# Attention and quantised feed-forward on one core: row maxima first in SyncE's list, stores and stack loads behind them and earlier, first stack in two halves, bulk loads issued by ScalarE

## The reference, cut to what matters

```python
# x, ctx: (16, 64, 256) f32; 8 heads of 8 channels; softmax over the 256 positions
def xattn(q, k, v, gamma):
    qh, kh, vh = (a.reshape(16, 8, 8, 256) for a in (q, k, v))
    qk = einsum('bhdq,bhdl->bhql', qh, kh) / sqrt(8)
    return gamma * einsum('bhql,bhdl->bhdq', softmax(qk), vh).reshape(16, 64, 256)

x = x + xattn(layernorm(x), ctx, ctx, gamma)          # k and v are both ctx
a = layernorm(x)                                      # (1024 rows, 256)
h = silu(bit_linear(a, w_gate)) * bit_linear(a, w_up) # (1024 rows, 1024)
h = rms_norm(h, ln_weight)
x = x + bit_linear(h, w_down)                         # (1024 rows, 256)
# bit_linear: activations rounded to 8 bits by their row's maximum,
# weights rounded to -1, 0, 1 by the mean of their absolute values
```

## Time and profile before

| what | value |
|---|---|
| median of 3 runs | 244.86 us (244.29 to 246.13) |
| span of the profiled execution | 248.6 us |
| busy PE, DVE, ACT, POOL | 178.4, 151.6, 140.9, 107.3 us |
| mean granted TensorE clock | 0.890 |
| DMA moved | 19.95 MB, mean 80 GB/s |

### The profile page before, as it was taken

The page is one execution under the profiler, slowest core; times in us unless marked ns, Lnnn a source line. Parts: engine busy times, 40 slices in busy tenths (PEclk is TensorE's granted clock), DMA queues, the critical chain, the costliest instruction groups (busy, mean ns, idle before and its releaser), DMA issues.

```text
span 248.6 us, 4308 instructions
## 1 busy us (share of the span) xinstructions
PE 178.4 (72%) x1370; PEld 103.8 (42%) x1378; DVE 151.6 (61%) x282; ACT 140.9 (57%) x286; POOL 107.3 (43%) x282
## 2 busy tenths in 40 slices
...
PEclk9999999996599997997569999965995699999689
...
GB/s 100 139 142 261 126 177 313 115 121 154 63 1 37 118 107 0 56 149 77 1 67 141 75 26 116 135 9 34 142 105 0 5 3 22 7 21 0 22 1 21
DMA packets 15871, 19.95 MB, mean 80 GB/s; under 512 B 2649, under 2 KB 14057, under 8 KB 14697
## 3 DMA queue, kind: packets, MB, share of 16 engines
...
## 4 chain that ended last, share of the span: by engine, by line
PE 33%; DMA 14%; DVE 7%; issue 6%; ACT 6%; POOL 4%; SPq 3%; POOLq 0%; ACTq 0%; DVEq 0%
DMA q_stack<-mt 13%; PE psO L463 9%; PE psB L447 7%; PE psA L433 6%; PE psG L565 2%; PE psG L505 2%; ACT probs L594 2%; PE psG L555 2%; POOL hw L325 2%; DVE mneg L736 1%; SPq L333 1%; ACT o_sb L629 1%; SPq L341 1%; DVE wgT L755 1%; DVE w_sb L747 1%
## 5 line engine op out<-in xcount | busy, mean ns | idle before, releaser
L736 DVE TENSOR_REDUCE mneg<-psA 128x2 f32<-128x512 f32 x128 | 82.7, 680 | 46.5 <-PE psA L433 46.4
L594 ACT ACTIVATE probs<-psB 128x512 f32<-128x512 f32 x128 | 74.0, 597 | 39.8 <-PE psB L447 39.7
L433 PE MATMUL psA<-k_stack,q_stack 72*128 72x256 bf16 x256 | 57.9, 319 | 23.1 <-DMA q_stack<-q_scratch 20.7
L447 PE MATMUL psB<-q_stack,k_stack 75*128 75x256 bf16 x256 | 55.2, 303 | 23.8 <-DMA q_stack<-mt 22.0
L463 PE MATMUL psO<-probs,vt 128*32 128x256 f32 x512 | 41.6, 451 | 1.0 <-ACT probs L594 1.0
L433 PEld LDWEIGHTS psA<-k_stack,q_stack 72*128 72x128 bf16 x256 | 23.9, 108 | 43.3 <-issue 30.1
L447 PEld LDWEIGHTS psB<-q_stack,k_stack 75*128 75x128 bf16 x256 | 25.7, 108 | 37.2 <-DMA q_stack<-mt 23.8
L325 POOL TENSOR_TENSOR hw<-h,lnw 128x512 f32<-128x512 f32 x15 | 19.1, 1270 | 39.3 <-DVE h L826 28.0
L463 PEld LDWEIGHTS psO<-probs,vt 128*32 128x32 f32 x512 | 14.8, 121 | 16.9 <-issue 9.9
L815 DVE SCALAR_TENSOR_TENSOR gu<-th,psG 128x512 f32<-128x512 f32 x15 | 10.3, 688 | 9.7 <-ACT th L657 9.7
L657 ACT ACTIVATE th<-psG,tscale 128x512 f32<-128x512 f32 x15 | 10.3, 688 | 9.1 <-PE psG L535 9.0
(11 more groups left out here) (129 smaller groups left out, 268.4 us busy)
## 6 DMA issues: line engine op xcount, KB each, us to landing
...
out_dram<-y_sb SPq DMA_DIRECT2D x8, 128.0 KB, 4.2
```

Of the source, the lines that this page charges most:

```text
L433: mm = pe.matmul(psA[n % A_BANKS][:, qt * L:(qt + 1) * L], q_stack[0:STACK, t % NBUF, bh, qt * P:(qt + 1) * P], k_stack[0:STACK, t % NBUF, ...
L447: mm = pe.matmul(psB[b % 2][:, lt * L:(lt + 1) * L], k_stack[:, t % NBUF, bh, lt * P:(lt + 1) * P], q_stack[:, t % NBUF, bh, :], start=Tru ...
L594: act.activation(probs[:, b % RING, :], psB[b % 2][:, :], ACT.Exp, scale=SCALE).then_inc(s_exp, 1)
L736: dve.tensor_reduce(mneg[:, k % MBUF, QT * (bh % HALF):QT * (bh % HALF + 1)], psA[n % A_BANKS][:, :].rearrange("p (q l) -> p q l", q=QT), ...
```

## The change

The table moves: parts and statistics of tile t are made 15 to 17 half-steps earlier, the stores go from m = -26 to -43 (17 earlier), the stack loads from -20 to -27 (7 earlier). On SP the maxima rows now come first in a half-step's code, so with the stores at 21 and the loads at 37 (modulo 32) each of the two stands right behind one DMA of maxima rows. The first stack is loaded in two halves of 8 heads, and PE starts on the first half. The bulk of x and ctx and the weights are issued by ACT at m = -6, -4, -2, 2, 6, the weights as one DMA each, all behind a wait for the whole first stack; the load of tile 1's stack waits for it too. `SP_LNW`, the load of the norm's weights, goes from 50 to 37.

```diff
-ACT_QK1, ACT_QK2, ACT_CTX, ACT_M, ACT_O, ACT_AQ, ACT_AT = -31, -25, 16, 20, 62, 79, 82
+ACT_QK1, ACT_QK2, ACT_CTX, ACT_M, ACT_O, ACT_AQ, ACT_AT = -48, -41, 16, 20, 62, 79, 82
-POOL_XHAT, POOL_QK1, POOL_QK3, POOL_M, POOL_RSTD = -29, -26, -19, 21, 71
+POOL_XHAT, POOL_QK1, POOL_QK3, POOL_M, POOL_RSTD = -46, -42, -35, 21, 71
-SP_STORE, SP_LOAD, SP_OUT = -26, -20, 119
-SP_W = (12, 13, 15, 17, 19, 22, 23, 25, 27, 29, 31, 33)
-SP_LNW = 50
+SP_STORE, SP_LOAD, SP_OUT = -43, -27, 119
+ACT_BULK = (-6, -4, -2, 2, 6)
+SP_LNW = 37
...
+        def load_first(eng, k, half):
+
+            heads = slice(half * HALF, (half + 1) * HALF)
+            done = (s_first, s_stack[0])[half]
+            for c in range(PARTS):
+                rows = slice(REP * c, REP * (c + 1))
+                if k == 0:
+                    eng.dma_start(k_stack[rows, 0, heads, :].rearrange("p b l -> p (b l)"),
+                                  k_scratch[0, :, c, heads].rearrange("d b l -> d (b l)").unsqueeze(1)
+                                  .to_broadcast([DH, PARTS, HALF * L])).then_inc(done, DMA)
+                else:
+                    eng.dma_start(q_stack[rows, 0, heads, :].rearrange("p b l -> p (b l)"),
+                                  q_scratch[0, :, :, heads].rearrange("d c b l -> (d c) (b l)")).then_inc(done, DMA)
...
-            load_q(sp, 0)
+            sp.wait_ge(s_qst[0], PARTS * DMA)
+            load_first(sp, 1, 0)
+            load_first(sp, 1, 1)
             sp.wait_ge(s_rows, 1)
             load_ones(sp, 0)
-            sp.dma_start(x_sb[:, 2:T, :], x_rows[2:T].rearrange("g p l -> p g l")).then_inc(s_x[2], DMA)
-            sp.dma_start(c_sb[:, 2:T, :], ctx_rows[2:T].rearrange("g p l -> p g l")).then_inc(s_c[2], DMA)
             for m in range(2 * FIRST, 2 * LAST):
                 n = m // 2
+                k = half_at(m, ACT_M)
+                if k is not None:
...
                 if t:
                     if t >= NBUF:
                         sp.wait_ge(s_b, BH * (t - NBUF + 1))
+                    if t == 1:
+                        sp.wait_ge(s_stack[0], 2 * PARTS * DMA)
...
-                if m in SP_W:
-                    sp.wait_ge(s_a, n + 1)
-                    load_w(*divmod(SP_W.index(m), 4))
...
-                    if i == 0:
+                    if n == 0:
+                        pe.wait_ge(s_first, 2 * PARTS * DMA)
+                    elif i == (0 if t else HALF):
                         pe.wait_ge(s_stack[t % NBUF], 2 * PARTS * DMA * (t // NBUF + 1))
...
-            load_k(act, 0)
+            for c in range(PARTS):
+                act.wait_ge(s_kst[c][0], DMA)
+            load_first(act, 0, 0)
+            load_first(act, 0, 1)
...
+                if m in ACT_BULK:
+                    j = ACT_BULK.index(m)
+                    if j == 0:
+                        act.wait_ge(s_first, 2 * PARTS * DMA)
+                        act.wait_ge(s_stack[0], 2 * PARTS * DMA)
+                        act.dma_start(x_sb[:, 2:T, :], x_rows[2:T].rearrange("g p l -> p g l")).then_inc(s_x[2], DMA)
+                    elif j == 1:
+                        act.dma_start(c_sb[:, 2:T, :], ctx_rows[2:T].rearrange("g p l -> p g l")).then_inc(s_c[2], DMA)
+                    else:
+                        src = (w_gate, w_up, w_down)[j - 2].rearrange("(c p) n -> p c n", p=P)
+                        act.dma_start(w_sb[:, j - 2, :].rearrange("p (c n) -> p c n", c=src.shape[1]), src).then_inc(s_w[j - 2], DMA)
```

More of the change, by code:

```diff
@@ L76 @@
 DVE_GU0, DVE_H0, DVE_GU1, DVE_H1, DVE_HMAX, DVE_OUT = 88, 88, 89, 90, 95, 113
-POOL_XHAT, POOL_QK1, POOL_QK3, POOL_M, POOL_RSTD = -29, -26, -19, 21, 71
+POOL_XHAT, POOL_QK1, POOL_QK3, POOL_M, POOL_RSTD = -46, -42, -35, 21, 71
 POOL_A, POOL_HW0, POOL_HW1, POOL_CR, POOL_H = 77, 97, 100, 100, 101
-SP_STORE, SP_LOAD, SP_OUT = -26, -20, 119
-SP_W = (12, 13, 15, 17, 19, 22, 23, 25, 27, 29, 31, 33)
-SP_LNW = 50
+SP_STORE, SP_LOAD, SP_OUT = -43, -27, 119
+ACT_BULK = (-6, -4, -2, 2, 6)
+SP_LNW = 37
 ACT_WS, WS_STEP, PE_W, DVE_W, POOL_WQ, DVE_WQ, WQ_STEP = 40, 4, 51, 51, 52, 54, 5
 PE_WB, WB_STEP, WB_LAG = 56, 2, 0
-POOL_INIT, DVE_STATS = 16, 14
+POOL_INIT, DVE_STATS = 16, 15
 BANK_CTX, BANK_M, BANK_OTR, BANK_RET, BANK_ATR, BANK_HTR0, BANK_HTR1, BANK_DOWN, BANK_W = 1, 1, 0, 0, 1, 0, 1, 0, 0
@@ L231, in build @@
         s_stack = [sem(f"stack_loaded{i}") for i in range(NBUF)]
+        s_first = sem("first_heads_loaded")
         s_a = sem("a_scores")
@@ L350, in _ @@
         def _(sp):
-            def load_w(k, j):
-                wide = w_sb[:, k, :].rearrange("p (c n) -> p c n", c=4)
-                if k < 2:
-                    rows = (w_gate, w_up)[k].rearrange("(j c p) n -> j p c n", c=2, p=P)[j]
-                    sp.dma_start(wide[:, j, :].rearrange("p (c n) -> p c n", c=2), rows).then_inc(s_w[k], DMA)
-                else:
-                    half = slice(512 * (j % 2), 512 * (j % 2 + 1))
-                    sp.dma_start(wide[:, j, :], w_down[P * (j // 2):P * (j // 2 + 1), half]).then_inc(s_w[k], DMA)
             for t in range(2):
@@ L366, in _ @@
                 store(sp, 0, 1, c)
-            load_q(sp, 0)
+            sp.wait_ge(s_qst[0], PARTS * DMA)
+            load_first(sp, 1, 0)
+            load_first(sp, 1, 1)
             sp.wait_ge(s_rows, 1)
             load_ones(sp, 0)
-            sp.dma_start(x_sb[:, 2:T, :], x_rows[2:T].rearrange("g p l -> p g l")).then_inc(s_x[2], DMA)
-            sp.dma_start(c_sb[:, 2:T, :], ctx_rows[2:T].rearrange("g p l -> p g l")).then_inc(s_c[2], DMA)
             for m in range(2 * FIRST, 2 * LAST):
                 n = m // 2
+                k = half_at(m, ACT_M)
+                if k is not None:
+                    t, half = divmod(k, 2)
+                    sp.wait_ge(s_mtsb, k + 1)
+                    sp.dma_start(q_stack[STACK:STACK_M, t % NBUF, half * HALF:(half + 1) * HALF, :]
+                                 .rearrange("c b (q l) -> c (b q) l", q=QT), mt[:, k % 2, :]).then_inc(s_mrow[half], DMA)
                 t = tile_at(m, SP_STORE)
@@ L393, in _ @@
                     sp.dma_start(gam[:, :], gamma.partition_broadcast(P)).then_inc(s_lnw, DMA)
-                k = half_at(m, ACT_M)
-                if k is not None:
-                    t, half = divmod(k, 2)
-                    sp.wait_ge(s_mtsb, k + 1)
-                    sp.dma_start(q_stack[STACK:STACK_M, t % NBUF, half * HALF:(half + 1) * HALF, :]
-                                 .rearrange("c b (q l) -> c (b q) l", q=QT), mt[:, k % 2, :]).then_inc(s_mrow[half], DMA)
                 u = tile_at(m, SP_OUT)
```

2 lines of the change are left out of this document (1 added, 1 removed).

## The result

The changed kernel takes 227.9 us at the median of four runs (227.26 to 228.64), the kernel before 245.5 us beside it (four runs, 244.29 to 248.23). The ratio is 0.929, with an interval of 0.924 to 0.934.

The account below looks back on a forecast made before the run. PE stalls for maxima rows queued behind stack loads, the clock falls after them, and a late start were taken as the bound. Gains 16.1 + 2.8 + 4.0 + 4.6 = 27.5 us took 248.6 to 221.1 profiled, 217.4 us timed; range 210 to 232.

Parts of the forecast that it names:

- Steady part, B0 of tile 2 to B0 of tile 6: Between these tiles' first pass B: moving stack loads off the maxima rows removes PE stops and clock falls, gaining 16.1 us.
- The give-back of 0.8 us per tile: Steady tiles: 0.8 us of each tile's gain deducted because other engines caught up during stops, with ACT and DVE at 89%.
- From B0 of tile 6 to the end: Last stretch, where nothing is loaded: only the clock comes back, 3.6 us less 0.8, a gain of 2.8 us.
- Between the first and the third B0: Between 42.59 and 93.87: the last stop's 3.16 us and about 0.8 us of ACT go, a gain of 4.0 us.
- The start: Up to the first pass B: maxima rows no longer queue behind weights, so it comes at 38.0 instead of 42.59, gaining 4.6 us.
- x would land late (27.5): At the start: x, issued only after the whole first stack, lands at 27.5 (bounds 22 and 31), delaying DVE's statistics.
- the rows would land in 2 to 3 us with no weights ahead: At the start: first maxima rows, issued at 35.2, land 2 to 3 us later instead of 9.9.
- The objection that the prediction named and set aside: At the start: transfers from several engines share the DMA engines, only issue time is saved, so the start comes no earlier.
- rival 2: At the start: bulk loads hold ACT or x lands late, first pass B at 46 to 48; 226 us, chance 0.12.
- From the profile to the timed runs: Whole kernel: timed runs lie 3.7 us below the profiled span, so 221.1 becomes 217.4 us.
- Rival 1: Steady tiles: the load still covers the maxima rows, each of five tiles keeping a 1.4 us stop; about 231 us, chance 0.12.
- Rival 3: Steady part: short idle spots keep PE's clock at the lower level; slower, about 267 us, chance 0.04.

Follow-up runs that it names:

- Experiment 5: Changed kernel with parts, statistics' use, stores and stack loads of tiles 2 to 7 at their old half-steps, new start kept; 250.63 us, ratio 1.002.
- experiment 7: Changed kernel with stack loads 2 half-steps earlier (-29 for -27), just ahead of the second half's maxima rows; 251.76 us.
- experiment 12: The best version (221.48 us) with tile 1's stack load and the bulk of ctx held until the first maxima rows have landed; 225.78 us, ratio 0.919.
- experiment 3: Changed kernel with ACT's weight loads and its conversions of tile 2, which need ctx, both behind its first copy of the maxima; 225.35 us, ratio 0.911.
- experiment 10: Changed kernel, weights late, tile 2 prepared late; ACT issues first rows, with ctx and other tiles' DVE and POOL work behind; 221.48 us, ratio 0.897.
- experiment 8: Kernel before the change, with all 16 maxima-row DMAs issued by ACT behind its copy instead of by SP; 255.47 us, ratio 1.039.
- experiment 1: Changed kernel with ACT's three weight loads moved behind its first copy of the maxima; 228.08 us, ratio 0.923.
- experiment 2: Changed kernel with ACT's two conversions of tile 2, which wait for ctx, behind its first copy of the maxima; 229.34 us, ratio 0.926.
- experiment 4: Changed kernel with weights behind the first maxima copy and tile 2's parts, stores and load at their old half-steps; 223.85 us, ratio 0.914.
- experiment 11: Changed kernel with weights late, tile 2 prepared late as before, and tile 1's stack load behind the first maxima rows on SP; 233.19 us, ratio 0.940.

## Why the prediction was right, and where it wasn't

Faster, and inside the range: 227.9 for a forecast of 217.4 (210 to 232). The mechanism of the large part held; the size was 10.5 us off (from median to median the gain is 17.6 us for a forecast of 27.5, and the median of before itself moved from 244.86 to 245.5). That it stays inside the range is owed to the width of the range. The chances add up to 0.92 for a gain of over 1%, not 0.94.

**Steady part, B0 of tile 2 to B0 of tile 6: held.** Forecast a gain of 16.1 us, measured 91.83 - 74.58 = 17.25 (B0 at 93.08 and 167.66). Forecast a tile of 18.9 us, measured 18.8, 18.9, 18.8 and 18.1, at a clock of 1.00. Experiment 5 takes just this part away and the ratio is 1.002, experiment 7 shows that the load's place does it. But both numbers are taken from the same long execution of the kernel before (see below): how much of the 17.25 us a median execution would have given, no trace shows.

**The give-back of 0.8 us per tile: somewhat too large.** Gaps and clock were 19.3 us and 17.25 of them came, so 0.5 us per tile was given back.

**From B0 of tile 6 to the end**: forecast 2.8, measured 62.90 - 58.44 = 4.46. **Between the first and the third B0**: forecast 4.0, measured 51.28 - 48.48 = 2.8.

**The start: this step failed.** Forecast 4.6 us gained, B0 at 38.0; measured 2.0 lost, B0 at 44.60, an error of 6.6 us. The step has three parts. That x would land late (27.5) was wrong: DVE's statistics start at 23.62, since x goes first on ACT's queue and took 5.1 us. That ACT has nothing else there until about 35, and is covered, was right as a sentence and wrong in use: with x early, the maxima are split at 30.30, and every us of ACT beyond is a us of B0. ACT is free for its copy only behind the two weight issues (7.40 and 7.81 us) and ctx at 35.8. I had priced such issues from the 3.03 us of a store; nearer rows stood in the same trace, SP's issues of weights, 11.34 us for seven of 256 KB:

```profile
33.46 4.91 SPq L356 DMA_DIRECT2D w_sb<-in_L_ffn_w_up_dram  x3
38.41 6.43 SPq L359 DMA_DIRECT2D w_sb<-in_L_ffn_w_down_dram  x4
```

And that the rows would land in 2 to 3 us with no weights ahead was wrong: 6.96 us, with the three weight loads in flight from the other queue (ctx had landed at 35.8). The 2.4 us exist in experiment 12, alone; in experiment 3, with ctx and the end of tile 1's stack in flight but no weights, it is 5.3. The objection that the prediction named and set aside, that another engine's queue changes nothing but the issue, was the better forecast: the start came no earlier. The row that it read as agreeing, 11.1 us for x, doesn't part the two queues, since x also stood behind the query stack on its own. The step as a whole is rival 2 in its mechanism ("if they hold ACT") with B0 at 44.60 instead of 46 to 48.

The sum of the profiled executions is then 2.8 + 17.25 + 4.46 - 2.0 = 22.5 us, 248.6 to 226.1, against 27.5 forecast: 5.0 of the 10.5 us.

**From the profile to the timed runs: this failed too, by 5.5 us.** I took the timed runs to lie 3.7 us below the span. In every execution that has both, the time is 1.8 us above its span (1.75 to 1.93): the changed kernel's four have spans of 226.1, 226.8, 225.4 and 226.1 for 227.91, 228.64, 227.26 and 227.89. So the profiled execution of before, with 248.6, was one of its long ones (by the same 1.8 us it'd be a time of 250.4, and 245.5 a span of 243.7). The 3.7 us weren't a difference between two clocks but the luck of one execution. The executions of before in all series spread over spans of 241.3 to 251.7, those of experiment 5 over 244.6 to 252.8, those of the changed kernel over 225.4 to 226.8: the wide spread is found where the stops are. Who takes the stops out may take the excess of that one execution out with them, and mustn't subtract it a second time from what is left.

**Rival 1** (the load still covers the rows) didn't come. The distance from one tile's last rows to the next tile's first was 9.2 us and not 8.6, and B0 came 4.26 us behind the issue (111.89 - 107.63). If the rows land as they did before, 10.8 to 11.6 us behind the load's first issue, the room was not 0.2 to 0.5 us but 1.0 to 1.8 in three of the four tiles (B0 12.6 us behind it) and 0.4 to 1.2 in the last. How little would have done it shows in experiment 7. **Rival 3** (the clock) didn't come either: in the clock line one slice is at 5 and one at 6, and the four stretches are at 1.00.

What stays open: why the rows took 13.0 us in experiment 10 and 5.3 to 8.2 in others (by the packet records they ended at 34.3 and tile 1's stack at 34.5, 14.7 us behind its first issue, so they may have waited for that load as in the steady part, but no run tests it); what slowed experiment 8; whether the clock's fall after 1.40 us and not after 1.37 lies in the stop or in what was around it; and what bounds the steady tile at 18.8 us, with PE busy 17.5, DVE 16.5 and ACT 16.2 (no run tried it).

## What to carry to other kernels

A small transfer that an engine waits for was here as slow as what was in flight with it. So look in the timeline for the last large issue ahead of it, and move that one so that it has landed by then, rather than the small one to another queue; but count who waits for the large one (10.27 us in experiment 12). When loads go to a compute engine's list, count how long their issue can hold it and what it would have been free for. And work a forecast from several executions where stops scatter: compare the profiled one with the median, and say which of its stops make the difference, before subtracting.

## What the runs showed that I hadn't expected

- The 12 KB of maxima rows took 2.4 us alone, 5.3 us beside ctx and the end of a stack load (experiment 3), 5.5 to 7.8 us beside a stack load on the same queue and 5.6 to 7.4 on the other, 6.1 to 8.2 us with weights in flight (the change, experiments 1, 2, 4 and 11), 9.95 us before (42.59 - 32.64) behind tile 1's stack and weights on one queue, and 13.0 us in experiment 10.
- An issue of a 1 MB load took 0.37 to 1.5 us in the experiments that issue it late (once 4.75, in experiment 4), and 6.17 to 9.08 us where x, ctx and another 1 MB had just been issued on the same queue.
- The 768 KB of ctx (rows of 1 KB) took 15.6 to 17.3 us behind x with tile 1's load (rows of 8 KB) issued beside them, 6.6 us behind x without that load, and 4.9 us with the load but without x ahead, while x, first on the queue, landed in 4.8 to 5.1 us in all of these.
- Moving the load by 7 half-steps past nothing did nothing (0.928 for 0.929); by 2 half-steps past one row DMA it undid the change.
- In experiment 5 the stretch behind a stop of 2.60 us was 4.6 us longer than one of the changed kernel (23.4 for 18.8); 1.66 of it is the next stop, so what the first cost again behind it, at a mean clock of 0.78, was by this estimate some 2.9 us, more than the gap itself.
